# Attention with an expert layer: output projection by pairs of heads, ten low parts a batch made on GpSimd

## The chip, the cores and the metric

One NeuronCore of a Trainium2 chip runs the whole kernel in one launch. The metric is the device time in microseconds, the median of several runs. A measurement of this kernel cannot tell a change of less than about 0.2% (3.4 us) from none.

## What is computed

Eight batches of 512 tokens with 256 features go through cross attention over 1024 context rows and then through a layer of experts:

```python
x = x + tanh(g0) * (softmax(q @ k.T / 8) @ v).concat_heads() @ Wo + bo   # q from layernorm(x), k and v from ctx; 8 heads of 64
x = x + tanh(g1) * moe(layernorm(x))     # router, top 2 of 8 experts with a capacity, gated silu, weighted scatter-add
```

(`tanh(g0)` multiplies the bias too.) Every float32 product is made of split operands: an operand t is a high part t_h (a copy rounded to the type fp32r) and a low part t_l = t - t_h, and a product is t_h u_h + t_h u_l + t_l u_h.

## The kernel before, in words

**Stages.** A short START makes the first k and q. Then one body for each of the 8 batches (FIRST, six MIDDLE, LAST), each of 32 steps. One step u is one unit: 128 tokens of one pair of heads, both heads of the pair in steps u and u+1. END finishes the last batch while the expert layer begins. The expert layer follows and is not touched by the change.

**One pair of steps.** TensorE (PE) makes the scores of units u and u+1 (`make_scores`, L1103, L1118). VectorE (DVE) takes the negative maximum (`highest`, L1931), ScalarE (ACT) the exponential with its sum (`exponent`, L1528). DVE takes the reciprocal (L2035), and GpSimd (POOL) scales the probabilities of both units (L918). Two steps later PE transposes them into one PSUM area of two banks, `turned` (`turn`, L1123, L1130). ACT copies each half as the high part pt_h (L1472), DVE subtracts for the low part pt_l (`low_turned`, L1708). The next `turn` waits for pt_l, since there is only one `turned`. So in an even step PE makes two sets of scores, one turn, the jobs of that step, and then the turn of the odd step, which waits for scores, two maxima on DVE and a pt_l.

**Jobs.** All other matmuls are jobs in a table written by hand (`JOBS`, L82, and `FIRST_JOBS` for the first batch): x and h are transposes, q, k and v projections, o probabilities times values (L1236), w the output projection (L1198 to L1205), l and r the router. Job number c writes one of two PSUM banks in turn (`ring`), so PE's job c waits until job c - 2 is drained. In the step after, ACT makes the high part (`drain`, L1486) and DVE the low part (`drain`, L1872), which frees the bank. In an even step all drains come first, in an odd step one drain, then the exponential or the reciprocal, then the others, then pt_h and pt_l. Every queue is in order.

**Values and projection.** v_hl holds for each head 64 high columns and 64 low columns side by side, so one o matmul gives v_h p in the upper 64 partitions of the bank and v_l p in the lower 64. ACT copies the upper half as ot_x[0:64] and the whole as ot_h. DVE puts the low part of the upper half in ot_x[64:128] (L1922). The projection w takes eight matmuls of 128x256 for a token block and half of the heads, two for a head: ot_h with wo_h and ot_x with wo_x. It is one of eight jobs a batch: w(0,j) in steps 16, 18, 20, 22 and w(1,j) in steps 0, 2, 4, 6 of the body after.

**Small work between.** DVE makes the layer norms (`layer`, L1720 to L1758) and the router (`route`, L1760 to L1839) in small operations, each at a place (step, gap) of `between` (L1949). L1746, L1750, L1753 and L1757 are steps 4 to 7 of a layer norm; L1757 releases the normalisation on POOL (L871). POOL also splits the context (L844, in steps 22 and 24), adds the bias (L955, step 14) and scatters the router's rows (L884, steps 29 and 30).

**Output weights.** wo comes in two halves (L633 to L644), each loaded twice for the two partition halves. ACT copies each twice (L1570 to L1575, steps 5 and 6 of FIRST), DVE subtracts each (L1998 to L2002, steps 7 and 8).

## Time and profile before

| | |
|---|---|
| median of 3 runs | 1711.11 us (1710.55 to 1712.54) |
| the profiled execution | 1709.52 us, of which its span 1707.8 us |
| granted TensorE clock, mean | 0.996 |
| busy, whole span | PE 96%, DVE 74%, ACT 61%, POOL 39% |
| FIRST, steps 0 to 31 | 21.3 to 159.0 us |
| one MIDDLE body | 129.15 us |
| attention ends, experts begin | about 1071 us |

The busy share of an engine is an average over the span; what a stage waits for is read from its own window. Matmul ends are modelled and overlap, so the start-to-start distance tells more than the duration.

### The profile page before, as it was taken

The numbers are of one execution on the slowest core, as the hardware profiler recorded it, in microseconds if no ns is written. First come the engines' busy times: TensorE is split into PE (matmuls) and PEld (weight loads), VectorE is DVE, ScalarE is ACT, GpSimd is POOL, SyncE is SP. The second block draws the span as 40 slices with busy tenths as digits, with TensorE's granted clock in tenths as the row PEclk, the third lists the DMA queues.
The fourth block names the chain that finished last, engine by engine and source line by source line (L and its number), as shares of the span: only waits on it lengthen the run. The fifth ranks groups of instructions, "written<-read, shape, count | busy, mean of one in ns | idle before, by whom it ended". The sixth has DMA issues, their size and how long they took to land.

```text
span 1707.8 us, 33525 instructions
## 1 busy us (share of the span) xinstructions
PE 1640.7 (96%) x12454; PEld 1494.2 (87%) x12454; DVE 1262.5 (74%) x2597; ACT 1048.9 (61%) x2179; POOL 672.5 (39%) x629
## 2 busy tenths in 40 slices
PE   6999999999999999999999998989999999999997
PEld 5788888888888888888888886889999999999997
DVE  6888888888888888888888878666565656547443
ACT  5767766666766767667766667536454555546443
POOL 3352444444345345345245334423343422332322
PEclk9999999999999999999999999999999999999999
DMA  4300210111121121031031032314423421341211
GB/s 127 125 26 1 93 71 26 76 75 39 56 96 38 36 106 48 15 124 51 13 125 39 14 137 72 134 42 110 115 39 108 113 37 29 109 115 29 38 33 27
DMA packets 60555, 115.49 MB, mean 68 GB/s; under 512 B 6616, under 2 KB 48480, under 8 KB 59776
## 3 DMA queue, kind: packets, MB, share of 16 engines
q1 hardware_dynamic: 37104, 79.24, 13.1%
q0 software_dynamic: 15392, 18.66, 6.1%
q10 hardware_dynamic: 7920, 15.73, 2.6%
q8 instruction: 88, 1.44, 0.3%
q14 instruction: 51, 0.42, 0.1%
HBM read 90.27 MB, written 57.42 MB: 86 GB/s over the span
## 4 chain that ended last, share of the span: by engine, by line
PE 73%; DVE 13%; issue 5%; POOL 4%; ACT 3%; DMA 2%; POOLq 0%; ACTq 0%; DVEq 0%; SPq 0%; another core or an unknown queue 0%
PE ring L1236 11%; PE turned L1130 10%; PE ffn L1093 10%; PE ffn L1095 10%; PE ffn L1094 10%; PE scores L1118 9%; DVE neg_max L1931 5%; PE ring L1093 3%; PE ring L1095 3%; PE ring L1094 3%; DVE pt_l L1708 3%; PE ring L1202 1%; DMA out<-y,y_token 1%; PE ring L1204 1%; POOL lists L884 1%
## 5 line engine op out<-in xcount | busy, mean ns | idle before, releaser
L918 POOL TENSOR_SCALAR probs<-probs,row_rec 128x1024 f32<-128x1024 f32 x254 | 282.3, 1124 | 465.9 <-DVE row_rec L2035 454.4
L1472 ACT ACTIVATE pt_h<-turned 128x512 fp32r<-128x512 f32 x512 | 278.7, 601 | 208.1 <-PE turned L1130 208.1
L1708 DVE TENSOR_TENSOR pt_l<-turned,pt_h 128x512 fp32r<-128x512 f32 x512 | 331.6, 680 | 6.4 <-ACT pt_h L1472 6.4
L1931 DVE TENSOR_REDUCE neg_max<-scores 128x1 f32<-128x1024 f32 x256 | 302.3, 1217 | 34.7 <-PE scores L1118 34.6
L1130 PE MATMUL turned<-ident,probs 128*128 128x128 f32 x2048 | 281.1, 279 | 27.0 <-DVE pt_l L1708 19.6
L1130 PEld LDWEIGHTS turned<-ident,probs 128*128 128x128 f32 x2048 | 223.9, 141 | 94.9 <-issue 61.6
L1528 ACT ACTIVATE probs<-scores,neg_max 128x1024 f32<-128x1024 f32 x256 | 285.3, 1116 | 13.8 <-DVE neg_max L1931 12.6
L1236 PE MATMUL ring<-pt_h,v_hl 128*128 128x256 f32 x1024 | 261.3, 293 | 0.8
L1236 PE MATMUL ring<-pt_l,v_hl 128*128 128x256 f32 x1024 | 250.7, 283 | 0.0
L2301 DVE TENSOR_TENSOR act_f<-ffn,silu 128x256 f32<-128x256 f32 (+1 forms) x232 | 108.4, 467 | 125.7 <-ACT silu L1642 114.8
L1236 PEld LDWEIGHTS ring<-pt_h,v_hl 128*128 128x128 f32 x1024 | 195.7, 191 | 4.9 <-issue 3.6
L1236 PEld LDWEIGHTS ring<-pt_l,v_hl 128*128 128x128 f32 x1024 | 196.6, 192 | 0.0
L1642 ACT ACTIVATE silu<-ffn 128x256 f32<-128x256 f32 (+1 forms) x232 | 97.0, 418 | 155.8 <-PE ffn L1095 135.3
L1023 POOL DMA_INDIRECT out<-y,y_token x62 | 100.4, 1620 | 180.1 <-DVE y L2233 169.1
L1472 ACT ACTIVATE act_h<-act_f 128x256 fp32r<-128x256 f32 (+1 forms) x232 | 105.1, 453 | 107.4 <-DVE act_f L2301 98.8
L1708 DVE TENSOR_TENSOR act_l<-act_f,act_h 128x256 fp32r<-128x256 f32 (+1 forms) x232 | 110.5, 476 | 72.5 <-ACT act_h L1472 67.2
L1093 PE MATMUL ffn<-w_h,act_h 128*128 128x256 f32 x544 | 155.9, 287 | 0.6 <-DVE act_l L1708 0.6
L1094 PE MATMUL ffn<-w_l,act_h 128*128 128x256 f32 x544 | 153.5, 282 | 0.0
L1095 PE MATMUL ffn<-w_h,act_l 128*128 128x256 f32 x544 | 153.1, 281 | 0.0
L1093 PE MATMUL ffn<-et_h,w_h 128*128 128x256 f32 (+1 forms) x464 | 141.4, 305 | 4.1 <-DVE act_f L2301 2.6
L1093 PE MATMUL ffn<-et_h,wg_h 128*128 128x256 f32 (+1 forms) x464 | 140.2, 302 | 0.9 <-issue 0.9
L1095 PE MATMUL ffn<-et_h,wg_l 128*128 128x256 f32 (+1 forms) x464 | 140.2, 302 | 0.0
(260 smaller groups left out, 3903.0 us busy)
## 6 DMA issues: line engine op xcount, KB each, us to landing
lists<-pads SPq DMA_DIRECT2D x8, 4160.0 KB
w_raw<-w_t ACTq DMA_DIRECT2D x10, 1024.0 KB, 8.7
e_rows<-lists SPq DMA_DIRECT2D x26, 390.0 KB
ctx_raw<-ctx_t SPq DMA_DIRECT2D x15, 512.0 KB, 3.8
wg_raw<-wg_t ACTq DMA_DIRECT2D x5, 1024.0 KB, 7.7
x_in<-x SPq DMA_DIRECT2D x8, 512.0 KB, 4.1
x_sum<-x SPq DMA_DIRECT2D x8, 512.0 KB, 3.9
out<-x_sum SPq DMA_DIRECT2D x8, 512.0 KB, 2.9
```

The costliest lines, as they stand in the source:

```text
L918: nc.gpsimd.tensor_scalar(probs[:, k, :], probs[:, k, :], row_rec[:, k:k + 1], 1.0, ALU.mult, ALU.mult).then_inc(scaled, 1)
L1093: nc.tensor.matmul(out_, sh, mh, start=start, stop=False)
L1094: nc.tensor.matmul(out_, sh, ml, start=False, stop=False)
L1095: return nc.tensor.matmul(out_, sl, mh, start=False, stop=stop)
L1118: last = nc.tensor.matmul(scores[:, ab, cols], st[head, buf, toks], mv[head, buf, cols], start=n == 0, stop=n == 2)
L1130: last = nc.tensor.transpose(turned[:, kt, :], probs[:, n % 4, kt * P:(kt + 1) * P], ident[:, :])
L1236: last = nc.tensor.matmul(bank[:, 0:2 * P], v_hl[:, kt, h, :], part[:, ab, kt, :], start=kt == 0 and part is pt_h, stop=kt == KT - 1 and p ...
L1472: return nc.scalar.activation(dst, src, ACT.Copy)
L1528: nc.scalar.activation(probs[:, k, :], scores[:, n % 2, :], ACT.Exp, bias=neg_max[:, k:k + 1], accum_out=row_sum[:, k:k + 1])\
L1708: return nc.vector.tensor_tensor(dst, src, hi_part.bitcast(F32), ALU.subtract)
L1931: nc.vector.tensor_reduce(neg_max[:, k:k + 1], scores[:, n % 2, :].rearrange("p (a c) -> p a c", a=2), AX.XY, ALU.max, negate=True).then_i ...
L2301: nc.vector.tensor_tensor(act_f[:, c % 2, cols], up_bank(c, 0, blocks), silu[:, cols], ALU.mult).then_inc(act_done, 1)
```

## The change

Four things change. **(1) The projection goes by pairs.** v_hl now holds for a pair of heads the columns high A, low A, low B, high B. An o job still makes 16 matmuls, but head A's result stands in the upper half of the bank and head B's in the lower, so that the two high parts of a pair fill the 128 rows of one ot_h. w becomes six matmuls (two pairs, three passes each) where it was eight. **(2) A sum moves to POOL.** ACT copies v_l p to o_low, DVE puts its low part in o_rest, and POOL adds the two into ot_l (`join_low`), once for two o jobs, in steps 0, 4, 8, ... behind the scaling of the probabilities; w waits for that sum. **(3) Ten low parts of k and v a batch** (of 8 k and 8 v) are no longer made by DVE: ACT copies the raw bank too, which frees it, and POOL subtracts (`low_of_job`) at fixed steps behind the scaling. **(4) wo** is loaded once, copied once by ACT and subtracted once by DVE (steps 5 and 7 of FIRST). In `FIRST_JOBS` the jobs w(0,j) stand a step later.

```diff
+POOL_LOWS = [("k", 1, 0), ("k", 1, 1), ("k", 2, 0), ("k", 2, 1), ("v", 1, 0), ("v", 1, 1), ("v", 1, 2),
+             ("v", 1, 3), ("v", 0, 0), ("k", 0, 0)]
+POOL_LOWS_AT = {2: [0], 4: [1], 10: [2], 12: [3, 4], 16: [5, 6], 18: [7], 26: [8, 9]}
+RAW_SLOT = [0, 1, 0, 1, 2, 3, 0, 1, 2, 3]
...
             def load_wo():
...
+                sp.wait_ge(weights_split, 3)
+                sp.dma_start(x_sum[:, :, :], wo.rearrange("(g p) d -> p g d", p=P))\
+                    .then_inc(raw_loaded[3], 16)
...
+            def join_low(body, u):
+                i = ((u - 6) // 4 * 2 + 1) % (2 * H)
+                part, m = i // 4 % 2, i // 2 % 2
+                toks = slice(m * 2 * P, (m + 1) * 2 * P)
+                o = ("o", i, 0)
+                wait_drained(pool, body, body.where[o] if u > 0 else body.before.where[o] - RING)
+                nc.gpsimd.tensor_tensor(ot_l[:, part, toks], o_rest[:, part, toks], o_low[:, part, toks],
+                                        ALU.add).then_inc(ot_done, 1)
+
+            def low_of_job(body, n):
+                kind, i, j = POOL_LOWS[n]
+                wait_drained(pool, body, body.where[POOL_LOWS[n]])
+                raw = raw_of_job[:, RAW_SLOT[n], :]
...
+                nc.gpsimd.tensor_tensor(dst, raw, hi_part.bitcast(F32), ALU.subtract)\
+                    .then_inc(lows_split, 1)
...
+                    if u == 0 and body.prev or u % 4 == 0 and body is not END and \
+                            (body.prev if u < 8 else body.own):
+                        join_low(body, u - 2)
+                    if body.prev and body.own:
+                        for n in POOL_LOWS_AT.get(u, ()):
+                            if POOL_LOWS[n] in body.where:
+                                low_of_job(body, n)
...
                     if body is END and u == 0:
 
                         pool.wait_ge(listed, 16 * 2 * QT * (B - 1))
-                        for p in FIRST_LOWS:
+                        for p in FIRST_LOWS[:LOWS_AHEAD]:
+                            low_first(p)
+                        join_low(body, 2)
+                        for p in FIRST_LOWS[LOWS_AHEAD:]:
                             low_first(p)
...
+                    if pair < 3:
+                        until(pe, lows_split, at(b - 1, len(POOL_LOWS), (0, 2, 4)[pair]))
...
+                        until(pe, lows_split, at(b - 1, len(POOL_LOWS), (-1, 8)[i // H]))
...
-                    o = ("o", H * i + H // 2 + 1 + j // 2 * 2, 0)
-                    reads = [body.before.where[o] - RING if i == 1 and j < 2 else body.where[o]]
+                    pe.wait_ge(ot_done, at(b - 1 if i == 1 else b, H, 4 * i + 3 + j // 2))
...
-                    for h in range(H // 2):
-                        head = i * (H // 2) + h
-                        nc.tensor.matmul(bank[:, 0:D], ot_h[:, h, toks], wo_h[:, head, :],
-                                         start=h == 0, stop=False)
-                        last = nc.tensor.matmul(bank[:, 0:D], ot_x[:, h, toks], wo_x[:, head, :],
-                                                start=False, stop=h == H // 2 - 1)
+                    for part in range(2):
+                        pair = 2 * i + part
+                        last = passes(bank[:, 0:D], (ot_h[:, part, toks], ot_l[:, part, toks]),
+                                      (wo_h[:, pair, :], wo_l[:, pair, :]), part == 0, part == 1)
...
-                    hi(ot_x[0:DH, h % 4, toks], bank[0:DH, 0:2 * P])
-                    last = hi(ot_h[:, h % 4, toks], bank[:, 0:2 * P])
+                    main, low = slice(ab * DH, (ab + 1) * DH), slice((1 - ab) * DH, (2 - ab) * DH)
+                    hi(ot_h[main, pair % 2, toks], bank[main, 0:2 * P])
+                    last = hi(o_low[main, pair % 2, toks], bank[low, 0:2 * P])
...
+                if body.lows_on_pool(what):
+                    n = POOL_LOWS.index(what)
+                    until(act, lows_split, at(body.b - 1, len(POOL_LOWS), RAW_FREE[n]))
+                    hi(raw_of_job[:, RAW_SLOT[n], :], bank).then_inc(drained[c % 2], 1)
...
-                        hi(wo_x[DH:P, part, :], wo_raw(half)[DH:P, :, :])
-                        hi(wo_h[:, part, :], wo_raw(half)).then_inc(raw_hi, 1)
+                    if body is FIRST and u == 5:
+                        act.wait_ge(raw_loaded[3], 16)
+                        hi(wo_h[:, :, :], x_sum[:, :, :]).then_inc(raw_hi, 1)
...
-                if kind == "h":
+                if kind == "h" or body.lows_on_pool(what):
                     return
...
-                    last = lo(ot_x[DH:P, h % 4, toks], bank[0:DH, 0:2 * P], ot_h[0:DH, h % 4, toks])
+                    last = lo(o_rest[main, pair % 2, toks], bank[main, 0:2 * P], ot_h[main, pair % 2, toks])
...
-                    if body is FIRST and u in (7, 8):
...
+                    if body is FIRST and u == 7:
+                        split_raw(3, x_sum[:, :, :], wo_l[:, :, :], wo_h[:, :, :])
```

`lows_on_pool` is true for the jobs of POOL_LOWS in the bodies MIDDLE and LAST.

## Rows read from the trace of the kernel before

**Rows 1.** Busy time by stretch: its us, then PE, PEld, DVE, ACT, POOL, clock, DMA, GB/s.

```profile
21.31:159.00 137.69, 130.81 (x976) 112.00 (x978) 112.79 (x177) 98.27 (x194) 53.38 (x55) 1.00 0.17 59
...
417.30:546.45 129.15, 126.75 (x966) 108.95 (x964) 110.39 (x219) 89.63 (x183) 58.22 (x57) 1.00 0.17 63
```

**Rows 2.** Waits of one middle batch, 439.5 to 568.6 us: total, times, longest.

```profile
POOL probs L918 <- DVE row_rec L2035: 52.2, 12, 6.7
...
PE turned L1130 <- DVE pt_l L1708: 1.6, 3, 0.7
```

**Rows 3.** Timeline of PE, step 2 of a middle batch: start, us, what.

```profile
557.43 0.28 PE L1202 MATMUL ring<-wo_h,ot_h 128*128 128x256 f32 x1
...
558.38 0.81 PE L1130 MATMUL turned<-ident,probs 128*128 128x128 f32 x6
```

**Rows 4.** Timeline of PE in step 16, and the turn of step 17.

```profile
481.56 0.28 PE L1204 MATMUL ring<-wo_x,ot_x 128*128 128x256 f32 x1
482.56 1.16 PE L1130 MATMUL turned<-ident,probs 128*128 128x128 f32 x8 [0.72 <-DVE pt_l L1708]
```

**Rows 5.** Timeline of PE in FIRST, steps 7 to 9, and one DVE operation there.

```profile
50.24 1.16 PE L1130 MATMUL turned<-ident,probs 128*128 128x128 f32 x8 [0.73 <-DVE pt_l L1708]
...
53.52 0.73 PE L1118 MATMUL scores<-k_h,q_h 64*128 64x512 f32 x4 [0.72 <-ACT probs L1528]
...
59.54 1.16 PE L1130 MATMUL turned<-ident,probs 128*128 128x128 f32 x8 [1.90 <-DVE pt_l L1708]
...
55.09 1.97 DVE L1708 TENSOR_TENSOR wo_x<-rows,wo_h 64x1024 fp32r<-64x1024 f32 x1
```

**Rows 6.** A POOL group (busy, mean ns); tile v_hl on ACT and DVE: min/median/max ns.

```profile
L855 POOL TENSOR_TENSOR ctx_l<-ctx_raw,ctx_h 128x512 fp32r<-128x512 f32 x28 | 35.5, 1288 | 1.2
...
L1472 ACT ACTIVATE v_hl<-ring x64: 582/600/627, 25.3 to 1001.8; 128x512 fp32r<-128x512 f32 x64
L1708 DVE TENSOR_TENSOR v_hl<-ring,v_hl x64: 671/691/694, 26.0 to 1002.4; 128x512 fp32r<-128x512 f32 x64
```

**Rows 7.** Timeline of POOL and PE at the start of a body, steps 0 and 1.

```profile
545.28 2.22 POOL L918 TENSOR_SCALAR probs<-probs,row_rec 128x1024 f32<-128x1024 f32 x2 [1.91 <-DMA lists<-rows,list_row]
...
547.38 0.37 PE L1202 MATMUL ring<-wo_h,ot_h 128*128 128x256 f32 x1
...
549.92 1.16 PE L1130 MATMUL turned<-ident,probs 128*128 128x128 f32 x8
```

**Rows 8.** One DVE line, min/median/max ns, and one DVE operation of END.

```profile
L1741 DVE TENSOR_SCALAR norm<-mean_var x16: 157/170/877, 7.0 to 1086.5; 128x4 f32<-128x4 f32 x16
...
1082.13 1.55 DVE L1708 TENSOR_TENSOR act_l<-act_f,act_h 128x256 fp32r<-128x256 f32 x1 [0.48 <-ACT act_h L1472]
```

**Rows 9.** Timeline of POOL, steps 16 and 17.

```profile
476.34 2.22 POOL L918 TENSOR_SCALAR probs<-probs,row_rec 128x1024 f32<-128x1024 f32 x2 [3.47 <-DVE row_rec L2035]
483.30 2.16 POOL L871 TENSOR_SCALAR x_in<-x_in,norm 128x256 f32<-128x256 f32 x4 [4.74 <-DVE norm L1757]
```

**Rows 10.** Timeline of DVE, steps 15 and 16.

```profile
478.25 0.32 DVE L1750 TENSOR_TENSOR norm<-norm 128x4 f32<-128x4 f32 x1
...
479.13 0.15 DVE L1753 SCALAR_TENSOR_TENSOR norm<-norm 128x4 f32<-128x4 f32 x1
479.46 2.36 DVE L1931 TENSOR_REDUCE neg_max<-scores 128x1 f32<-128x1024 f32 x2 [0.17 <-PE scores L1118]
```

**Rows 11.** Timeline of POOL and PE, steps 11 and 12.

```profile
458.94 2.16 POOL L871 TENSOR_SCALAR rows<-x_sum,norm 128x256 f32<-128x256 f32 x4 [5.12 <-issue]
461.08 2.21 POOL L918 TENSOR_SCALAR probs<-probs,row_rec 128x1024 f32<-128x1024 f32 x2
...
462.25 1.10 PE L1130 MATMUL turned<-ident,probs 128*128 128x128 f32 x8 [0.45 <-POOL probs L918]
```

**Rows 12.** Timeline of PE, the turn of step 25.

```profile
516.62 1.37 PE L1130 MATMUL turned<-ident,probs 128*128 128x128 f32 x8 [0.36 <-DVE pt_l L1708]
```

**Rows 13.** Timeline of POOL at the start of END.

```profile
1071.03 1.12 POOL L909 TENSOR_SCALAR probs<-probs,row_rec 128x1024 f32<-128x1024 f32 x1 [1.83 <-DVE row_rec L2035]
```

More of the change, by code:

```diff
@@ L203, in of, with lows_on_pool @@
         return Body(b, self.prev, self.own, self.nxt, self.offset, FIRST if b == 1 else self.before)
+    def lows_on_pool(self, job):
+        return self.prev and self.own and job in POOL_LOWS
     def route_from(self):
@@ L386, in build @@
         small_loaded = sem("small_loaded")
-        raw_loaded = [sem(f"raw_loaded{i}") for i in range(5)]
+        raw_loaded = [sem(f"raw_loaded{i}") for i in range(4)]
         consts = sem("consts")
@@ L405, in build @@
         filled = sem("filled")
+        ot_done = sem("ot_done")
+        lows_split = sem("lows_split")
         drained = [sem("drained0"), sem("drained1")]
@@ L496, in whole @@
             return t[:, :, :].rearrange("p c n -> p (c n)")
-        def wo_raw(half):
-            return x_sum[:, :, :] if half == 0 else rows[:, :, 0:D]
         def first_ctx_raw(half):
@@ L633, in load_wo @@
             def load_wo():
-                for half in range(2):
-                    if half == 0:
-                        sp.wait_ge(weights_split, 3)
-                    else:
-                        sp.wait_ge(first_pads, 16)
-                    for copy_ in range(2):
-                        sp.dma_start(wo_raw(half)[copy_ * DH:(copy_ + 1) * DH, :, :],
-                                     wo[half * (INNER // 2):(half + 1) * (INNER // 2), :]
-                                     .rearrange("(h p) d -> p h d", p=DH))\
-                            .then_inc(raw_loaded[3 + half], 16)
+                sp.wait_ge(weights_split, 3)
+                sp.dma_start(x_sum[:, :, :], wo.rearrange("(g p) d -> p g d", p=P))\
+                    .then_inc(raw_loaded[3], 16)
                 sp.wait_ge(weights_split, 4)
@@ L886, in scatter @@
                     rows[:, q, :], None).then_inc(listed, 16)
+            def join_low(body, u):
[10 more added lines that the diff above has]
+                raw = raw_of_job[:, RAW_SLOT[n], :]
+                if kind == "k":
+                    keys = slice(j * 512, (j + 1) * 512)
+                    dst, hi_part = k_l[:, i % 2, keys], k_h[:, i % 2, keys]
+                if kind == "v":
+                    part = v_hl[:, i, 2 * j:2 * j + 2, :, :, :].rearrange("p t g s d -> p (t g) s d")
+                    dst, hi_part = part[:, :, 1:3, :], part[:, :, 0:4:3, :]
+                    raw = raw.rearrange("p (g a d) -> p g a d", a=2, d=DH)
+                nc.gpsimd.tensor_tensor(dst, raw, hi_part.bitcast(F32), ALU.subtract)\
+                    .then_inc(lows_split, 1)
             def low_first(p):
@@ L1232, in do_job @@
                 if kind == "o":
-                    h, ab = i // 4 * 2 + i % 2, i % 2
+                    pair, ab = i // 4, i % 2
                     for kt in range(KT):
+                        values = v_hl[:, pair // 2, kt, pair % 2, 2 * ab:2 * ab + 2, :]\
+                            .rearrange("p s d -> p (s d)")
                         for part in (pt_h, pt_l):
-                            last = nc.tensor.matmul(bank[:, 0:2 * P], v_hl[:, kt, h, :],
-                                                    part[:, ab, kt, :],
+                            last = nc.tensor.matmul(bank[:, 0:2 * P], values, part[:, ab, kt, :],
                                                     start=kt == 0 and part is pt_h,
@@ L1569, in step @@
                             .then_inc(tanh_done, 1)
-                    if body is FIRST and u in (5, 6):
-                        half = u - 5
-                        part = slice(half * 4, half * 4 + 4)
-                        act.wait_ge(raw_loaded[3 + half], 16 * 2)
-                        hi(wo_x[DH:P, part, :], wo_raw(half)[DH:P, :, :])
-                        hi(wo_h[:, part, :], wo_raw(half)).then_inc(raw_hi, 1)
+                    if body is FIRST and u == 5:
+                        act.wait_ge(raw_loaded[3], 16)
+                        hi(wo_h[:, :, :], x_sum[:, :, :]).then_inc(raw_hi, 1)
             def start():
```

45 lines of the change are left out of this document (23 added, 22 removed).

## The prediction

> **What bounds it now.** I read the busy time by batch first. Six middle batches take 129.15 us each, and PE is busy for 126.75 of them, against 110.39 on DVE, 89.63 on ACT and 58.22 on POOL [rows 1]. The waits of such a batch say the same: PE waits for pt_l 1.6 us in all, while POOL waits over 50 us for its next reciprocals [rows 2]. So PE is the bound, and POOL has room. But the room is not even. In the timeline, a projection job of eight matmuls starts at 557.43 and the turn behind it at 558.38, with nothing between [rows 3]: there a shorter job is time won. In step 16 the last matmul of the projection starts at 481.56 and the next turn only at 482.56, after a wait for pt_l [rows 4]: there the chain scores, two maxima, pt_l is the bound, and PE work in front of it is free. The other thing to see is that POOL and DVE disturb each other. L1741 works on 128x4 numbers in 0.17 us, yet took up to 0.877, and act_l took 1.55 us, where a subtraction of twice its size takes 0.69 [rows 6, 8]. In both cases a POOL operation ran, and DVE's ended with POOL's or right behind it.
>
> **The sum, part by part.** The profiled execution has 1709.5 us, 1.6 below the median of 1711.1. I make the sum against it and add 1.6 at the end.
>
> (a) **Two matmuls fewer in a w job.** Eight take 558.38 - 557.43 = 0.95 us [rows 3], so 0.119 each and 0.24 a job. 64 jobs: 15.2 us if PE were the bound everywhere. It is not: at step 16 nothing is won [rows 4], and at step 0 the turn at 549.92 stands on pt_l as well as on the job before [rows 7]. The jobs in steps 4 and 20 have only some 0.2 before the same chain binds. I take 1.3 us for each of the 7 batches behind FIRST, 0.8 for the four jobs of FIRST, 0.5 in END: **-10.4**. Bounds 0 and -15.2.
>
> (b) **The weights wo.** The second copy pair of ACT and the second subtraction of DVE go away in FIRST. PE waited 0.72 us for an exponential behind the copies and 1.90 us for a pt_l behind the subtraction of 1.97 us [rows 5], and 0.73 two steps earlier, also behind such copies [rows 5]. One copy and one subtraction stay, in steps that have room. **-3.5**; bounds 0 and -4.
>
> (c) **Ten lows off DVE.** 10 x 0.69 us a batch [rows 6]. I give this nothing: where PE waits for pt_l, none of the ten stands in front of the maxima. The chain of step 16 starts as the scores arrive, at 479.46 [rows 10]. Bounds 0 and -2 a batch (the PE waits there are, 1.6, with what lies around them [rows 2]).
>
> (d) **Ten raw copies on ACT.** 10 x 0.60 us a batch [rows 6], beside PE's work, since ACT has 39 us free. But in odd steps the copy stands in front of pt_h, which shifts pt_l by 0.60 less what DVE's own subtraction held it, some 0.3 to 0.4. Hidden in most steps by the next scores and an o job; in steps 12 and 16 it reaches the maxima. It is counted in (f) and (g).
>
> (e) **The sum in front of w, step 0.** POOL's scaling there comes late, behind the scatters: it starts at 545.28 and takes 2.22, so both units are scaled at 547.50. The first of them releases the turn, and w starts at 547.38, in front of the second one's end [rows 7]. Now w waits for scaling and sum. The sum is 128x256 in size; half of a 128x512 subtraction of 1.29 [rows 6] is 0.65, with a start cost some 0.75. So w starts at 548.3, 0.9 later. Less the 0.24 of the shorter job, and less the little time that there was, the turn of 549.92 comes 0.5 later. The body behind FIRST has no scatters in front. 6 x 0.5 = **+3.0**; bounds 0 and 6. Queued behind this wait are a k job and everything else of PE. At steps 4, 16 and 20 the sum is ready before w starts.
>
> (f) **Low parts on POOL against the layer norm, steps 9 to 12.** The low part of k(2,0) runs on POOL right behind the scaling of step 10, and L1746 comes at that moment. As read above, a small DVE operation on SBUF data waits until POOL's is over, up to 1.29 us. L1746, L1750 and the maxima slip, then L1757, and behind it the chain that PE already waits for: normalisation at 458.94, scaling at 461.08, turn at 462.25 after a wait of 0.45 [rows 11]. Every delay of L1757 goes into that turn. Between 0 and 1.2; I take 0.8 with the raw copies, 7 bodies: **+5.6**.
>
> (g) **Steps 15 and 16.** POOL's scaling runs from 476.34 to 478.56, and then it had nothing until 483.30 [rows 9]. Now the sum and two lows fill 478.6 to 481.9. In that stretch DVE has L1750, q_l and L1753 right in front of the maxima at 479.46 [rows 10]. L1750 already lasts 0.32 and not 0.16, ending with the scaling. Pushed by the raw copy to 478.6, it waits for the sum (to 479.3); L1753 then waits for the low part of v(1,1), to 480.6. The maxima start 1.25 later, in the one chain where PE has nothing to hide it [rows 4]. If L1753 slipped in between, 0.36 of the raw copy would be left. 6 bodies: **+7.5**; bounds 2 and 9. FIRST has the sum but no lows: +0.4.
>
> (h) **Steps 24 to 28.** The sum in step 24 shifts the split of the context by 0.75, so its last subtraction still runs when L1797 comes, in front of the pt_l that the turn at 516.62 waits for [rows 12]: +0.7. In steps 26 and 28 a low part and a sum meet router operations in front of the maxima: 0.3 each. 6 x 1.3 = **+7.8**; bounds 0 and 12.
>
> (i) **END.** The scaling of the last unit ends at 1072.15 [rows 13]. w(1,0) started before that and now waits for the sum behind it: **+1.2**. The sum for w(1,2) stands behind five weight splits of 1.3 us and is still in time.
>
> New waits of PE on lows_split: each low part is made 3 or more steps before its reader, at no cost. The queue of SP loses three of its four wo loads.
>
> Sum: -10.4 - 3.5 + 3.0 + 5.6 + 7.5 + 0.4 + 7.8 + 1.2 = **+11.6**, so 1721.1 for the profiled execution and **1722.7** for the median.
>
> The Trainium skill, page "SBUF — State Buffer", section "Who interferes with whom", says that a DVE instruction with two SBUF inputs and a GpSimd one that reads SBUF exclude each other for the whole instruction, whoever issues first. By that rule L1753, L1797 and L1822 are exposed and the maxima, a `tensor_reduce`, never are; taken at its fullest it is Rival 4 below.
>
> **The rivals.**
>
> Rival 1, **faster, the meetings miss the path**. DVE gets in between two POOL operations, or the freed 6.9 us a batch let it arrive early. Then (f) to (h) shrink to the raw copies' 0.36 in two steps, 7 x 0.7 = 5, and the sum is -10.4 - 3.5 + 3.0 + 5 + 1.2 = -4.7: 1706.4. The point from which it decides lies within 0.1 us: L1750 issued before 478.56 meets only the end of the scaling, as now [rows 9, 10]. Against it: with the raw copy it comes at about 478.6, and L1753 comes some 0.9 later in either case, while POOL is still busy.
>
> Rival 2, **PE is the bound throughout**. The lows off DVE also shorten the chain, all of (a) and (b) is won: -18.7, so 1692.4. Against it: the waits of steps 17 and 25 have no k or v subtraction in front [rows 4, 12].
>
> Rival 3, **gains and meetings cancel**: half of (f) to (h) is 10.4 less, within 0.2%: about 1712.
>
> Rival 4, **each meeting costs a whole POOL operation**. Six a batch at 1.29 us [rows 6] are 7.7 us and not the 3.4 of (f) to (h): 6 x 4.3 = 26 more, 1749. Likewise if a low part of v, with its pattern of 64 columns, took 2.4 us and not 1.29. Against it: the collisions that the rows show cost only the rest of POOL's operation, 0.16 at L1750 and up to 0.71 at L1741 [rows 8, 10].
>
> That the job is not shorter (the three passes at a slower pace) I hold for excluded: k and v jobs of the same form keep 0.12 us.
>
> **The numbers.** The forecast case has 0.50; with Rival 4 at 0.04, slower by over 0.2% is 0.54. Rival 1 has 0.27 and Rival 2 has 0.06: faster is 0.33. Within 0.2% is 0.13. The forecast case alone, with its bounds, covers 1715 to 1731. The range reaches down to Rival 1 and leaves out Rivals 2 and 4 and the far bounds: 1703 to 1731.
>
> **What would show it.** Right: w jobs 0.70 us long; L1753 in step 16 at over 0.5 us, and a wait for pt_l of 1.5 us or more in front of the turn of step 17; the turn of step 12 waiting for POOL by over 1 us; w(1,0) released by the sum; a middle batch of about 131.3 us and a FIRST of about 134 us. Wrong: L1750 and L1753 at 0.16 us, a middle batch of 129 us or less. If a middle batch comes out under 128 us, the view that DVE's relief buys nothing, (c), is what failed.

## The result, and the profile after

The changed kernel takes **1739.09 us** (median of 4 runs, 1736.94 to 1740.07), against 1711.05 for the kernel before (1710.55 to 1712.54): a ratio of 1.0161, 95% interval 1.0143 to 1.0178. It is slower, as forecast, but by 28 us where 11.6 were forecast, and outside the range of 1703 to 1731. The profiled execution has a span of 1738.4 us, 30.6 more than before.

First a correction to what stands above. A MIDDLE body of the kernel before is not 129.15 us long. Measured from the first maximum of one batch (L1931) to that of the next, the six take 131.36 to 131.73 us, 131.5 in the mean; 129.15 was worked out with the last store, which comes earlier in END. FIRST is 129.27 us long by the same measure, not 137.7. All bodies below are measured from maximum to maximum, L1931 before and L1972 after.

The busy time by stretch, in the columns of [rows 1]: a middle batch of the kernel before,

```profile
284.00:415.40 131.40, 129.01 (x985) 111.11 (x982) 112.74 (x222) 91.27 (x185) 59.32 (x58) 1.00 0.16 62
```

and of the changed kernel FIRST, two middle batches, the sixth middle batch, and LAST up to its last maximum:

```profile
22.90:152.40 129.50, 122.57 (x908) 103.87 (x908) 105.04 (x168) 92.57 (x180) 55.06 (x59) 1.00 0.16 58
152.40:288.70 136.30, 129.62 (x968) 110.76 (x967) 110.54 (x212) 99.05 (x195) 76.98 (x76) 0.99 0.16 59
424.80:560.90 136.10, 129.72 (x969) 110.74 (x967) 110.19 (x212) 98.95 (x195) 77.41 (x76) 0.99 0.16 60
832.90:967.30 134.40, 127.88 (x966) 108.93 (x965) 110.00 (x211) 98.83 (x195) 76.84 (x76) 1.00 0.15 57
967.30:1096.40 129.10, 116.55 (x874) 100.17 (x874) 98.96 (x189) 93.98 (x182) 63.30 (x61) 0.97 0.19 74
```

DVE is 2.5 us less busy a batch, and the batch is longer by over 4 all the same. Five of the six have a clock of 0.99 and take 136.1; the one with 1.00 takes 134.4. The 30.6 us lie here: the six middle batches +25.8 (forecast: +15.3), FIRST +0.2 (forecast: -3.9), LAST +2.6 (forecast: -0.5), START, END and the rest +2.0 (forecast: +0.7).

**Step 16.** The timeline of DVE, POOL and PE in the changed kernel, against [rows 4, 9, 10]; L1790 and L1793 are L1750 and L1753 of before:

```profile
489.36 0.65 DVE L1790 TENSOR_TENSOR norm<-norm 128x4 f32<-128x4 f32 x1
489.93 0.68 DVE L1949 SCALAR_TENSOR_TENSOR q_l<-ring,q_h 128x512 fp32r<-128x512 f32 x1
490.53 0.71 DVE L1793 SCALAR_TENSOR_TENSOR norm<-norm 128x4 f32<-128x4 f32 x1
491.17 2.34 DVE L1972 TENSOR_REDUCE neg_max<-scores 128x1 f32<-128x1024 f32 x2
...
489.26 0.73 POOL L897 TENSOR_TENSOR ot_l<-o_rest,o_low 128x256 fp32r<-128x256 f32 x1
489.95 2.51 POOL L912 TENSOR_TENSOR v_hl<-raw_of_job,v_hl 128x512 fp32r<-128x512 f32 x2
...
494.25 1.62 PE L1169 MATMUL turned<-ident,probs 128*128 128x128 f32 x8 [2.19 <-DVE pt_l L1748]
495.53 0.56 PE L1275 MATMUL ring<-pt_h,v_hl 128*128 128x256 f32 x1
495.89 0.42 PE L1275 MATMUL ring<-pt_l,v_hl 128*128 128x256 f32 x1
...
498.46 0.28 PE L1275 MATMUL ring<-pt_h,v_hl 128*128 128x256 f32 x1
```

L1790 ends with the sum, at 490.0, and L1793 ends with the first low part of v. PE's wait for pt_l grows from 0.72 to 2.19. What nobody had forecast stands behind it. The o matmuls start 0.21 us apart until 498.2 and 0.12 apart after that. The clock records show the granted clock at 1.2 GHz from 494.8 for 3.41 us, and at 2.4 before and after; PE had stood idle for these 2.19 us and had begun again 0.5 us before the clock fell. Such a stretch lies in this place in the first five middle batches, none in the sixth, none in the middle batches of the kernel before.

**Steps 10 to 12, 24 and 25, and END.** DVE, POOL and PE again:

```profile
463.85 1.20 DVE L1786 SCALAR_TENSOR_TENSOR norm<-norm 128x4 f32<-128x4 f32 x1
...
463.74 1.29 POOL L912 TENSOR_TENSOR k_l<-raw_of_job,k_h 128x512 fp32r<-128x512 f32 x1
...
472.56 0.66 PE L1169 MATMUL turned<-ident,probs 128*128 128x128 f32 x4 [1.01 <-POOL probs L945]
...
528.93 0.77 DVE L1837 TENSOR_TENSOR oh<-rev,gate 128x32 f32<-128x32 f32 x1
...
527.11 2.55 POOL L857 TENSOR_TENSOR ctx_l<-ctx_raw,ctx_h 128x512 fp32r<-128x512 f32 x2
...
530.45 1.37 PE L1169 MATMUL turned<-ident,probs 128*128 128x128 f32 x8 [0.84 <-DVE pt_l L1748]
...
426.15 0.39 PE L1130 MATMUL ring<-wo_h,ot_h 128*128 128x256 f32 x1 [0.51 <-POOL ot_l L897]
...
1101.67 0.39 PE L1130 MATMUL ring<-wo_h,ot_h 128*128 128x256 f32 x1 [1.59 <-POOL ot_l L897]
```

A meeting, here and below, is a DVE operation that lasts longer while a GpSimd operation runs beside it. The meetings and waits of the forecast are there: L1786 (L1746 before) held for 1.20 us by the low part of k(2,0), and the turn of step 12 waiting 1.01 for POOL against 0.45 [rows 11]; L1837 (L1797 before) held until the split ends at 529.66; w(1,0) waiting for the sum at step 0 and in END.

### The profile page after: what moved, and what is told of

Read it like the earlier page. It is cut to its first block, busy times and chain, and to the rows that moved or that the text cites. A ratio compares the mean times of both kernels' runs of the same rounds, so it can differ in the third digit from the quotient of the medians.

```text
span 1738.4 us, 33457 instructions
## 1 busy us (share of the span) xinstructions
PE 1641.9 (94%) x12326; PEld 1486.5 (86%) x12326; DVE 1240.4 (71%) x2528; ACT 1101.4 (63%) x2244; POOL 800.8 (46%) x761
## 4 chain that ended last, share of the span: by engine, by line
PE 64%; DVE 14%; ACT 8%; POOL 7%; issue 5%; DMA 2%; ACTq 0%; POOLq 0%; DVEq 0%; another core or an unknown queue 0%; SPq 0%
PE ffn L1130 10%; PE ffn L1132 10%; PE ffn L1131 10%; PE ring L1275 10%; PE turned L1169 8%; PE scores L1157 6%; DVE neg_max L1972 4%; DVE pt_l L1748 4%; ACT probs L1571 3%; PE ring L1130 3%; PE ring L1132 2%; PE ring L1131 2%; POOL probs L945 2%; POOL lists L886 2%; ACT pt_h L1510 1%
## 5 line engine op out<-in xcount | busy, mean ns | idle before, releaser
L1169 PE MATMUL turned<-ident,probs 128*128 128x128 f32 x2048 | 285.5, 281 | 44.2 <-DVE pt_l L1748 30.9
L1972 DVE TENSOR_REDUCE neg_max<-scores 128x1 f32<-128x1024 f32 x256 | 302.0, 1215 | 26.8 <-PE scores L1157 26.6
L1275 PE MATMUL ring<-pt_h,v_hl 128*128 128x256 f32 x1024 | 267.0, 298 | 0.4
L1275 PE MATMUL ring<-pt_l,v_hl 128*128 128x256 f32 x1024 | 256.1, 287 | 0.0
L1275 PEld LDWEIGHTS ring<-pt_h,v_hl 128*128 128x128 f32 x1024 | 200.0, 195 | 3.4 <-issue 2.9
L1275 PEld LDWEIGHTS ring<-pt_l,v_hl 128*128 128x128 f32 x1024 | 200.8, 196 | 0.0
L1047 POOL DMA_INDIRECT y_weight<-weights_of,y_at x62 | 61.3, 989 | 178.4 <-DVE y_at L2307 155.5
```

Source lines behind the costliest of these rows:

```text
L1169: last = nc.tensor.transpose(turned[:, kt, :], probs[:, n % 4, kt * P:(kt + 1) * P], ident[:, :])
L1275: last = nc.tensor.matmul(bank[:, 0:2 * P], values, part[:, ab, kt, :], start=kt == 0 and part is pt_h, stop=kt == KT - 1 and part is pt_l)
L1972: nc.vector.tensor_reduce(neg_max[:, k:k + 1], scores[:, n % 2, :].rearrange("p (a c) -> p a c", a=2), AX.XY, ALU.max, negate=True).then_i ...
```

## The experiments

All times against the kernel before on the same chip. "Batch" is the mean of the six middle batches, worked out from the starts of their first maxima; "attention" is the start of the very last maximum, which leaves the expert layer out; "1.2 GHz" counts the middle batches with a stretch of 3.4 us at that clock. The edits are shown by their main lines; where GpSimd's operations are taken out, PE's waits for them go as well. A run that leaves a part of the product out says so in its text.

| run | us | ratio, 95% interval | batch | attention | 1.2 GHz |
|---|---|---|---|---|---|
| before | 1708.9 to 1712.8 | | 131.52 | 1067.8 | 0 |
| changed | 1739.09 | 1.0161 (1.0143 to 1.0178) | 135.82 | 1096.4 | 5 |
| e1_projection_only | 1724.54 | 1.0069 (1.0052 to 1.0086) | 133.09 | 1078.3 | 0 |
| e2_pool_writes_only | 1721.14 | 1.0049 (1.0032 to 1.0065) | 132.80 | 1077.2 | 0 |
| e3_tiny_raw | 1812.20 | 1.0576 (1.0558 to 1.0593) | 132.58 | 1075.2 | 0 |
| e4_w_behind_dve | 1736.04 | 1.0138 (1.0121 to 1.0155) | 135.43 | 1093.8 | 4 |
| e5_v_lows_at_18 | 1727.89 | 1.0097 (1.0078 to 1.0117) | 133.97 | 1084.3 | 0 |
| e6_k_low_at_12 | 1738.11 | 1.0148 (1.0127 to 1.0169) | 135.28 | 1092.1 | 4 |
| e7_both_moved | 1729.17 | 1.0101 (1.0082 to 1.0119) | 133.72 | 1083.5 | 0 |
| e8_before_maximum_twice | 1721.66 | 1.0058 (1.0037 to 1.0080) | 132.90 | 1079.6 | 1 |
| e9_short_low_copy | 1727.24 | 1.0109 (1.0094 to 1.0125) | 134.40 | 1086.2 | 2 |
| e10_pairs_alone | 1710.64 | 1.0011 (1.0002 to 1.0020) | 131.79 | 1071.4 | 0 |
| e11_unshifted_low_copy | 1817.57 | 1.0637 (1.0620 to 1.0653) | 135.04 | 1091.4 | 3 |
| e12_pairs_alone_first_as_before | 1707.25 | 0.9991 (0.9982 to 1.0000) | 131.79 | 1069.0 | 0 |
| e13_sum_on_dve | 1721.79 | 1.0070 (1.0057 to 1.0084) | 133.04 | 1080.3 | 0 |
| e14_sum_on_dve_lows_moved | 1734.71 | 1.0142 (1.0127 to 1.0158) | 135.26 | 1093.9 | 3 |
| e15_pairs_alone_short_copy | 1703.17 | 0.9956 (0.9943 to 0.9968) | 131.06 | 1061.6 | 0 |
| e16_join_behind_split | 1741.31 | 1.0184 (1.0167 to 1.0200) | 135.87 | 1096.3 | 5 |

### GpSimd's reads, the raw copies, or the wait of w?

e1, all low parts back on DVE:

```diff
-        return self.prev and self.own and job in POOL_LOWS
+        return False
```

> The paired projection with its sum on GpSimd stays; all sixteen low parts of k and v are subtracted on DVE again, and ACT makes no raw copies. Theory A (the loss of a middle batch, 131.4 to 136.1 us, comes from GpSimd's operations and DVE's small ones holding each other up, in steps 10 and 16 to 28, and from a stretch of TensorE at half clock in step 18 that follows the longer idle time of step 16): the meetings with low parts go, those with the sum stay, the half clock stretch goes, batch near 131.5 us, 1706 to 1716 us. Rival R (the raw copies on ACT delay pt_h, and that is the loss): the same 1706 to 1716, but then the run with tiny raw copies shows it too. Rival W (w behind the sum is the loss): stays above 1730.

e2, fills in place of GpSimd's subtractions and sums:

```diff
-                nc.gpsimd.tensor_tensor(dst, raw, hi_part.bitcast(F32), ALU.subtract)\
-                    .then_inc(lows_split, 1)
+                idle(384)          # three fills of scratch, 128x128
+                nc.gpsimd.memset(dst.bitcast(F32), 0.0).then_inc(lows_split, 1)
```

> GpSimd's ten subtractions a batch and its sums are replaced by fills that read nothing, several in a row so that GpSimd is busy about as long; all waits stay. It leaves out the low parts of ten k and v jobs and the low part of the attention output. Theory A (GpSimd's reads of SBUF and DVE's small operations hold each other up): batch 131 to 133 us, no stretch at half clock in step 18, 1708 to 1720 us. Rival Q (it is GpSimd's queue: its operations come late and with them the scaling and the sum): as the changed kernel, above 1733 us. Rival R (raw copies on ACT): above 1733 us too, since they stay.

e3, almost no raw copy:

```diff
-                    hi(raw_of_job[:, RAW_SLOT[n], :], bank).then_inc(drained[c % 2], 1)
+                    hi(raw_of_job[:, RAW_SLOT[n], 0:8], bank[:, 0:8]).then_inc(drained[c % 2], 1)
```

> ACT copies 8 columns of each of the ten raw banks and not 512, about 0.2 us in place of 0.6; GpSimd's subtractions are as long as before. The ten low parts are made from a constant, so they are wrong. Theory A: step 10 and step 16 win some 0.3 each, 0.6 x 6 = 4, so 1733 to 1737 us if the half clock stretch stays, and some 9 less, about 1725, if the smaller idle time of step 16 lets it go. Rival R (the raw copies are the loss): 1706 to 1716 us.

e4, w behind DVE:

```diff
-                    pe.wait_ge(ot_done, at(b - 1 if i == 1 else b, H, 4 * i + 3 + j // 2))
+                    o = ("o", H * i + H // 2 + 1 + j // 2 * 2, 0)
+                    reads = [body.before.where[o] - RING if i == 1 and j < 2 else body.where[o]]
```

> w waits for DVE's subtraction, as before, and reads its result in place of the sum; the sum still runs on GpSimd and nobody waits for it. It leaves the low half of the values out of the projection. Theory A: FIRST wins 3 to 4 us (TensorE waits there 1.5 us for the sum before w(0,0) and w(0,2), with what follows), a middle batch 0.3 to 0.5, END 1: 1731 to 1735 us. Rival W (the wait of w for the sum is the loss): 1706 to 1716 us.

Rival W fell at once: without the wait for the sum the batch is 0.4 us shorter, and over half of that is one stretch at 1.2 GHz fewer; batches of the same kind differ by 0.1. In FIRST, where 3 to 4 us had been forecast, nothing is won, since PE waits for DVE instead. Rivals Q and R fell with e2, at 1721. But e1, e2 and e3 each gave 2.7 to 3.2 us of the 4.3 back, a batch of 132.6 to 133.1, although e2 keeps the raw copies and e3 keeps GpSimd's ten subtractions. Theory A had the batch of e2 right (131 to 133); for e1 it had forecast 131.5 (1706 to 1716 us, measured 1724.5), and for e3 much less of a gain. (The time of e3 as a whole, and that of e11 below, says nothing, which its expectation missed: other values in k and v send other tokens to the experts, PE makes 12660 matmuls and not 12326, and 75 us of that layer run at 1.2 GHz. Only their attention counts.) The timelines of step 16 show that both the copy and the subtraction are needed for the loss there. In e2, DVE, then POOL:

```profile
483.10 0.15 DVE L1800 TENSOR_TENSOR norm<-norm 128x4 f32<-128x4 f32 x1
483.17 0.68 DVE L1959 SCALAR_TENSOR_TENSOR q_l<-ring,q_h 128x512 fp32r<-128x512 f32 x1
483.77 0.15 DVE L1803 SCALAR_TENSOR_TENSOR norm<-norm 128x4 f32<-128x4 f32 x1
...
482.98 0.47 POOL L897 MEMSET scratch<- 128x128 f32 x2
483.39 0.31 POOL L908 MEMSET ot_l<- 128x256 f32 x1
483.64 0.73 POOL L897 MEMSET scratch<- 128x128 f32 x3
```

and in e3:

```profile
481.27 0.36 DVE L1792 TENSOR_TENSOR norm<-norm 128x4 f32<-128x4 f32 x1
481.55 0.68 DVE L1951 SCALAR_TENSOR_TENSOR q_l<-ring,q_h 128x512 fp32r<-128x512 f32 x1
482.15 0.19 DVE L1795 SCALAR_TENSOR_TENSOR norm<-norm 128x4 f32<-128x4 f32 x1
...
481.59 0.74 POOL L897 TENSOR_TENSOR ot_l<-o_rest,o_low 128x256 fp32r<-128x256 f32 x1
482.28 2.51 POOL L912 TENSOR_TENSOR v_hl<-raw_of_job,v_hl 128x512 fp32r<-128x512 f32 x2
```

Beside fills both small operations take 0.15 us. In e3 they come early enough: the first meets only the end of the scaling and the second the end of the sum, and it is issued ahead of the low part of v. So the loss of step 16 is a product of two parts, the raw copy that makes DVE late and GpSimd's operation that reads; taking away either is enough. That is what Rival 1 of the prediction describes, and it comes about once the raw copy is gone.

The Trainium skill, page "SBUF — State Buffer", section "Who interferes with whom", says that a DVE instruction with two SBUF inputs contends with GpSimd's reads and not with a GpSimd instruction that only writes. By that rule the fills are harmless, and the traces agree: 0.15 us beside a fill, 0.71 and 1.20 beside a subtraction.

### Moving the low parts, and the stretch at 1.2 GHz

e5, e6 and e7 change the table alone:

```diff
-POOL_LOWS_AT = {2: [0], 4: [1], 10: [2], 12: [3, 4], 16: [5, 6], 18: [7], 26: [8, 9]}
+POOL_LOWS_AT = {2: [0], 4: [1], 12: [2, 3, 4], 18: [5, 6, 7], 26: [8, 9]}
```

e5 moves the two of step 16, e6 that of step 10, e7 both as shown.

> The low parts of v(1,0)'s neighbours, v(1,1) and v(1,2), run on GpSimd in step 18 in place of step 16; raw copies and waits as in the changed kernel. Theory A (they meet L1790 and L1793 in front of the maxima of step 16; the longer idle time there is followed by TensorE's stretch at half clock): a middle batch loses 1.0 to 1.2 at step 16 and 1.45 at step 18 in batches 1 to 5: 1722 to 1727 us. Rival R (the raw copies alone delay step 16; GpSimd's place does not matter): 1736 us or more. Rival C (the half clock stretch has nothing to do with step 16): 1731 to 1734 us, with the stretch still there.

> The low part of k(2,0) runs on GpSimd in step 12 in place of step 10. Theory A: the chain of the layer norm is no longer held in steps 9 to 12, a middle batch loses 0.84 us at step 11 and keeps the rest: 6 or 7 x 0.84 = 5 to 6, so 1733 to 1734 us. Rival R (the raw copy on ACT is what delays step 10 to 12): 1738 us or more. If the three low parts in a row at step 12 make the next scaling late, some of it comes back at step 14.

> Both moves together. Theory A: the sum of the two, a middle batch of 132.5 to 133 us as with the tiny raw copies or without the low parts: 1716 to 1721 us. Rival R: above 1733 us.

e8 adds to the kernel before:

```diff
+                    if body.own and body.prev and u == 16:
+                        v.wait_ge(scores_done, at(b, UNITS, u + 1))
+                        nc.vector.tensor_reduce(
+                            spare_max[:, :], scores[:, u % 2, :].rearrange("p (a c) -> p a c", a=2),
+                            AX.XY, ALU.max, negate=True)
```

> The kernel before, with one addition: in step 16 of every batch with a batch before it, DVE makes the first maximum twice (1.21 us more of DVE's time in front of the maxima that TensorE waits for). Theory A (a longer idle time of TensorE in step 16 is followed by a stretch at half clock whatever causes it): a middle batch grows by about 1.2 for the delay and by about 1.45 for the stretch, 7 x 1.2 + 5 or 6 x 1.45 = 16 to 17 us, so 1726 to 1729 us. Rival C (the stretch comes from something else of the changed kernel): no stretch, 6 to 8.5 us, 1717 to 1720 us.

e5 won 1.85 us a batch: 0.6 in step 16 (L1793 is back at 0.15; L1790 still meets the sum and takes 0.65) and all five stretches at 1.2 GHz. Its 1727.9 us lie just above the range of Theory A, and Rivals R and C are refuted. e6 won some 0.8 in steps 10 to 12 and gave 0.4 back by step 13, behind the three low parts in a row, and had one stretch fewer; its time as a whole, 1738.1 us where 1733 to 1734 were forecast, cannot be told from the changed kernel's. e7, forecast at 1716 to 1721, came out at 1729: the moves do not add up, since step 16 keeps the meeting with the sum and step 13 loses.

e8 prices the clock by itself. Two middle batches of e8, without and with a stretch, and PE's turn of step 17 in the latter:

```profile
286.00:418.60 132.60, 129.08 (x985) 111.13 (x983) 113.88 (x222) 91.36 (x185) 59.36 (x58) 1.00 0.16 61
551.20:685.20 134.00, 130.49 (x985) 112.67 (x984) 113.93 (x223) 91.44 (x185) 59.48 (x58) 0.99 0.16 61
```

```profile
619.53 1.62 PE L1131 MATMUL turned<-ident,probs 128*128 128x128 f32 x8 [1.86 <-DVE pt_l L1709]
```

The second maximum costs 1.14 us in each of the seven batches, to a few hundredths, and nothing of it is won back. In the fourth middle batch and in LAST a stretch follows and costs 1.46 more. Theory A had forecast five or six stretches and Rival C none, so the time of 1721.7 us lies between the two. A stretch in this place thus needs nothing of the changed kernel but a longer wait; but a wait is not always followed by one. By PE's wait in front of the turn of step 17, with the batches that had a stretch there: 0.7 us in the kernel before 0 of 7 (LAST counted); 1.6 to 1.7 in e5 and e7 0 of 12; 1.9 in e8 2 of 7 (LAST counted); 2.0 in e9 2 of 6; 2.1 in e11 3 of 6; 2.2 in the changed kernel, e4, e6 and e16 18 of 24. What decides in a single batch was not found. Nor is such a wait all that can come before a stretch: e14 has three of them from step 19 on, and in the 14 us before each of these PE never waited longer than 1.0 us. What leads to those is open.

### What the pairs cost and give by themselves

e9, e10, e11 and e12 split the projection's own part:

```diff
-                    last = hi(o_low[main, pair % 2, toks], bank[low, 0:2 * P])
+                    last = hi(o_low[main, pair % 2, m * 2 * P:m * 2 * P + 8], bank[low, 0:8])     # e9
+                    last = hi(o_low[main, pair % 2, toks], bank[main, 0:2 * P])                   # e11
```

e10 is the changed kernel without any low part or sum on GpSimd: w reads o_rest, DVE's result, and waits for DVE.

```diff
-                        last = passes(bank[:, 0:D], (ot_h[:, part, toks], ot_l[:, part, toks]),
+                        last = passes(bank[:, 0:D], (ot_h[:, part, toks], o_rest[:, part, toks]),
```

> The changed kernel, with ACT's copy of the low rows of an o result cut from 256 columns to 8. It leaves the low half of the values out of the projection. In the kernel before, ACT's two copies of an o result took 0.28 + 0.26 us from start to start in front of the next exponential; in the changed one they take 0.39 + 0.40, 16 times a batch. Theory O (these 0.25 us stand in the chain of the steps with an o result and eat what the shorter w jobs give): the gaps of +0.24 behind the w jobs of steps 7 and 23 and at 4, 13 and 29 go, a middle batch is 1.0 to 1.5 us shorter, with the stretch at half clock or without it: 1729 to 1733 us with it, 1722 to 1726 without. Rival P (the copies are hidden, and those gaps have another cause, GpSimd's sum above all): 1737 us or more.

> Nothing of the change on GpSimd and no raw copies: w reads DVE's result and waits for DVE, there is no sum. It leaves the low half of the values out of the projection. What stays is the w job of six matmuls, the wo load of one copy, the other order of the w jobs in FIRST, and the two copies of an o result. Theory O: a middle batch of 132.0 to 132.5 us, still above the 131.4 of before, since the copies cost more than the shorter w jobs give; 1714 to 1719 us. Rival S (the sum on GpSimd is what the rest of the loss comes from): a middle batch of 130.0 or less, 1698 to 1704 us.

> The changed kernel, with the copy of the low rows taken from the same partitions that it writes to (so the low half of the values is replaced by a second helping of the main rows, which is wrong). Theory O1 (the copy is slow to follow since it moves data to other partitions): 0.28 us from copy to copy, 1729 to 1733 us. Rival O2 (it is the form, two copies of 64 partitions in place of one of 64 and one of 128): 0.39 us as before this edit, 1737 to 1741 us.

> As the run with the pairs alone, and w(0,0), w(0,1) and w(0,2) of FIRST stand in steps 15, 16 and 19 as in the kernel before. Theory F (the later places, which the sum forces, put w jobs in front of the turns that wait for the longest chain): FIRST, that ends no earlier than before in the changed kernel although 3.5 us were won at step 8, wins 2 to 3.5 us: that much less than the pairs alone. Rival (FIRST takes the 3.5 back anyway, at steps that wait for DVE): the same time as the pairs alone within 1 us.

The copies of an o result on ACT, in the kernel before and in the changed one:

```profile
441.74 0.38 ACT L1472 ACTIVATE ot_x<-ring 64x256 fp32r<-64x256 f32 x1 [0.17 <-PE ring L1236]
442.02 0.36 ACT L1472 ACTIVATE ot_h<-ring 128x256 fp32r<-128x256 f32 x1
442.28 1.10 ACT L1528 ACTIVATE probs<-scores,neg_max 128x1024 f32<-128x1024 f32 x1
```

```profile
451.22 0.38 ACT L1510 ACTIVATE ot_h<-ring 64x256 fp32r<-64x256 f32 x1 [0.17 <-PE ring L1275]
451.61 0.38 ACT L1510 ACTIVATE o_low<-ring 64x256 f32<-64x256 f32 x1
452.02 1.11 ACT L1571 ACTIVATE probs<-scores,neg_max 128x1024 f32<-128x1024 f32 x1
```

The durations are alike, but the next one starts after 0.28 and 0.26 us before, after 0.39 and 0.41 now: 0.26 us later for the exponential behind it, 16 times a batch. In e11 the second copy follows after 0.28, and the exponential still after 0.39: so O1 and O2 are both half right. The move to other partitions is 0.11 of it, and the rest comes with a copy of 64 partitions right in front of the exponential. That copy also writes another type than before (f32, not fp32r), but e13 below rules the type out: there a copy of 64 partitions to fp32r is the last one, and the exponential still starts 0.40 after it.

```profile
444.71 0.38 ACT L1502 ACTIVATE ot_h<-ring 64x256 fp32r<-64x256 f32 x1 [0.17 <-PE ring L1267]
445.11 1.12 ACT L1562 ACTIVATE probs<-scores,neg_max 128x1024 f32<-128x1024 f32 x1
```

e9 shows what the copy costs: a batch is 1.4 shorter than the changed kernel's (part of that are three stretches fewer), and its batches without one take 133.5 to 134.2 against 134.4. That is less than Theory O had said: the gaps at steps 7 and 23 stayed.

e10 is the run on which the argument turns. Nothing of the change is left on GpSimd, every w job is 0.23 us shorter than before (0.72 from its start to the turn behind it, 0.95 before), and the batch takes 131.79, 0.3 more than before:

```profile
284.50:416.30 131.80, 128.38 (x969) 109.35 (x970) 112.32 (x221) 94.09 (x185) 59.63 (x58) 1.00 0.17 62
```

All that eight shorter jobs give is taken back in other steps of the same batch. Both theories missed this run: O had 1714 to 1719 us, S 1698 to 1704, and it took 1710.6.

FIRST is told apart by e10 and e12. The first maxima of its batch and of the next lie 129.27 us apart before, 129.48 in the changed kernel, 128.91 in e10 and 126.71 in e12, whose FIRST is here in the columns of [rows 1]:

```profile
23.90:150.60 126.70, 121.60 (x907) 104.03 (x908) 104.80 (x167) 92.53 (x180) 50.83 (x53) 1.00 0.16 60
```

So the 3.5 us won at step 8 are real, and the places that the sum forces on w(0,0), w(0,1) and w(0,2) cost 2.2 of them, as Theory F of e12 had said, and the sum itself 0.6.

### Can the chain be helped?

e13 and e14 let DVE make the sum, from PSUM:

```diff
-                    last = lo(o_rest[main, pair % 2, toks], bank[main, 0:2 * P], ot_h[main, pair % 2, toks])
+                    lo(o_rest[low, pair % 2, toks], bank[main, 0:2 * P], ot_h[main, pair % 2, toks])\
+                        .then_inc(rest_done, 1)
+                    v.wait_ge(rest_done, at(b, hi_events["o"], n + 1))
+                    last = nc.vector.tensor_tensor(ot_l[main, pair % 2, toks], bank[low, 0:2 * P],
+                                                   o_rest[low, pair % 2, toks], ALU.add)
```

> The whole computation. All low parts of k and v on DVE; the low rows of an o result are not copied by ACT: DVE subtracts as before and then adds the low rows from PSUM itself (16 operations of about 0.42 us more a batch). No sum on GpSimd; the w jobs of FIRST stand as in the kernel before. Theory O (ACT's copies and the sum on GpSimd are what the pairing costs): ACT's 0.40 us per o result go, at most 0.42 of DVE come in behind pt_l, a middle batch of 130.9 to 131.8, 1700 to 1709 us. Rival D (DVE's 6.7 us a batch more stand in the chain of pt_l and the maxima): a middle batch above 132.5, 1715 us or more.

> The whole computation. As the run with the sum on DVE, with the ten raw copies and GpSimd's ten low parts back, those of step 16 in step 18 and that of step 10 in step 12. Theory O: the raw copies on ACT cost 0.6 us and more a batch at steps 12 and 16, DVE's relief gives some of it back (0.15 at step 8, 0.35 at step 24): 0 to 1 us a batch above the run with the sum on DVE, 1702 to 1714 us. Rival D (DVE is what the sum on DVE loads too much): faster than that run by 3 us or more.

> The pairs alone with FIRST as before, and ACT's copy of the low rows of an o result cut to 8 columns. It leaves the low half of the values out of the projection. Theory O (the copies eat the gain of the w jobs): a middle batch 0.9 to 1.3 us shorter than with the full copy, 130.5 to 130.9, 1698 to 1702 us. Rival T (the chain that ends in pt_l binds in those steps whatever ACT's copies take): 131.5 to 131.8, 1705 to 1708 us.

> The changed kernel, with the sum of step 24 behind GpSimd's two operations of the context's split in that step instead of in front of them. Theory A: the second subtraction of the split ends 0.7 us earlier, L1839 and the pt_l behind it are no longer held, TensorE's wait behind the second k job of step 25 goes: 0.5 us less there, against 0.35 gained behind it that may go too; a middle batch 0.2 to 0.5 shorter: 1736 to 1738 us. Rival (the sum does as much harm behind the split): 1739 us or more.

Both complete versions, e13 and e14, are slower than the kernel before. e13 takes 133.0 us a batch: ACT's relief is there (88.1 us busy against 94.1 in e10), but DVE has 120.1 against 112.3, and the sum stands in front of pt_l, with gaps of 0.3 to 0.6 in steps 3, 7, 19 and 23. Rival D was right on e13. On e14, which relieves DVE, it was wrong, and Theory O with its 1702 to 1714 us too: the raw copies are back, and with them 2.2 us a batch, 0.7 of it three stretches at 1.2 GHz. e15 takes 131.06, 0.73 less than the pairs alone: with the copies out of the way the pairs gain 0.46 a batch over the kernel before, of the 1.84 that their jobs are shorter. Its 1703.2 us lie between Theory O and Rival T, so the copies are part of what takes the gain back, and not all of it. It leaves a part of the product out, and still wins only 0.44%. No complete version that beats the kernel before was found.

e16 shows the meeting of step 24 from the other side. DVE, then POOL:

```profile
528.19 0.75 DVE L1839 TENSOR_TENSOR oh<-rev,gate 128x32 f32<-128x32 f32 x1
528.87 0.68 DVE L1750 TENSOR_TENSOR pt_l<-turned,pt_h 128x512 fp32r<-128x512 f32 x1
...
525.66 2.54 POOL L857 TENSOR_TENSOR ctx_l<-ctx_raw,ctx_h 128x512 fp32r<-128x512 f32 x2
528.16 0.73 POOL L897 TENSOR_TENSOR ot_l<-o_rest,o_low 128x256 fp32r<-128x256 f32 x1
```

The split now ends at 528.2, as the operation comes, but the sum starts 0.03 us ahead of it and holds it just as long. The batch is as long as the changed kernel's, so the rival of e16 was right.

## Why the prediction was right, and where it failed

The forecast had the sign, the places and the mechanism of the meetings, and missed the size by 16 us. Its worst step is (a), the gain from shorter w jobs. Its sum for a middle batch is +2.55, which on the true length of 131.5 gives 134.1 and on its own base 131.7; the 131.3 that it names is a slip. The one middle batch without a stretch took 134.4. But that closeness is in part luck: (a) was too good by 1.6 a batch, and against it (e) and (h) were too dear by 0.25 and 0.7 and the relief of (c) was left out. Per middle batch, from start to start on PE:

- **(a) failed, and is the largest miss.** Eight jobs are 0.23 us shorter each, as read from [rows 3]. The step from there to -1.3 a batch is wrong: e10 has all eight, none of the meetings, and is 0.3 longer than before. The argument "nothing stands between the job and the turn, so a shorter job is time won" looks at the next instruction only. The turn that moves up finds the same POOL, ACT and DVE behind it, and at steps 5, 7, 13 and 23 PE then waits 0.2 to 0.3 within that step. And the change makes the chain longer: the two copies of an o result are 0.26 us slower to follow, a term that the ledger did not have. e10 and e15 part the two: with the low copy cut short the pairs give 0.46 a batch and not 1.3, and the full copy costs 0.73. In the six middle batches -7.8 became +1.6.
- **The clock was not in the sum.** Five stretches of 1.46 us (the price from e8) are 7.3. The forecast had said that PE's wait in step 16 would grow, and asked only what the wait costs, not what PE does after it.
- **(b) right, then lost.** FIRST wins 3.5 by step 8 (PE's gaps there shrink by 0.5, 0.8, 2.1 and 0.1). The later places of the w jobs, of which the prediction says nothing, take 2.2 back (e10, e12).
- **(c) small, but not nothing**: with the ten subtractions off DVE e3 is 0.5 a batch shorter than e1 (132.58 and 133.09), though it still has their meetings and ten small copies. So the relief is worth 0.5 or more, within the bounds of 0 and 2.
- **(d)** has no run of its own. At step 16 the raw copy costs under 0.2 us where GpSimd's operations do not read (e2), and without it the meeting does not come about (e3).
- **(e)** was 0.25 and not 0.5: w(1,0) starts 0.75 later, and by the maxima of step 2 all but 0.1 to 0.4 of it is made up. In e4, without the wait, they come as early as before.
- **(f), (g) right to 0.1**: 0.8 forecast and some 0.83 measured in steps 10 to 12; 1.25 forecast and 1.2 measured in step 16. L1793 at 0.71, PE's wait at 2.19 and the turn of step 12 at 1.01 lie beyond the marks that were named beforehand. e6 and e5 show that they go with the low parts.
- **(h) right in kind, half the size.** L1837 is held for 0.6 us, as forecast. PE waits 0.5 more, and wins 0.35 back a few operations later, since two low parts are off DVE at step 24. With 0.4 at steps 28 and 29 it is some 0.6 and not 1.3.
- **(i) right**: w(1,0) of END waits 1.59 us for the sum, 1.2 forecast.

Rival 2 had -18.7. It is refuted by e10, where nothing meets and (a) and (b) are there in full, and the kernel is no faster than before; e3, which also has the lows off DVE, is slower per batch. Rival 4 is refuted by the size of each meeting. The sum of what the parts cost a middle batch: the pairs 0.3 (e10), the sum on GpSimd 1.3 (e1 less e10), low parts with raw copies 1.3 (the batch without a stretch, 134.4, less e1), the stretches 1.4 in the mean; together 4.3, which is 135.82 less 131.52. Of the sum's 1.3, 0.6 arises at steps 24 and 25 and 0.4 at steps 28 and 29, by the maxima of e1 against e10; which meetings these are no run shows one by one. Of the 2.6 us in LAST, 0.8 is the meeting of step 10, and 1.0 arises at step 30, where a stretch at 1.2 GHz is 3.4 us longer than before. e10 has that longer stretch and the 1.0 too; what makes it longer is open.

## What to carry to other kernels

A shorter job on the busiest engine is time won only if the work behind it can also move up; try it alone, with everything else of the change taken out, before it gets a term in the sum. When an operation goes to an idle engine, look at what the move itself adds to the others (a raw copy, a wait, a later place in a table): here these cost more than the relief, and two small delays that are harmless by themselves cost 1.25 us together. And a wait of the matmul engine of some 2 us may be paid for twice, in the wait and in the clock after it.

## What was not expected of the hardware

- After a wait of TensorE of about 2 us the granted clock was at 1.2 GHz for 3.41 us, in 18 of 24 batches with a wait of 2.2 us and in 2 of 7 with 1.9, at a price of 1.46 us each (e8). In e14 three such stretches came with no wait above 1.0 us in the 14 us before.
- ACT's next instruction started 0.28 and 0.26 us after the start of a copy of 256 columns in the kernel before, and 0.39 and 0.41 after it in the changed one, though each lasts 0.36 to 0.38. Copying to other partitions than those read was 0.11 of that (e11); the type written made no difference (e13).
- A small DVE operation on SBUF takes 0.15 us beside fills of GpSimd and up to 1.20 beside a subtraction; q_l, which reads one operand from PSUM, keeps its 0.68 beside both.
